# Edge buckets of 250 destinations instead of 417, and a new order at the seam of query stage, mask and first attention

## The chip, the cores and the metric

The kernel runs on one core of a Trainium2 chip. A core has four compute engines that run side by side and meet at semaphores: TensorE (PE, matmuls; PEld is its weight load), VectorE (DVE), ScalarE (ACT) and GpSimd (POOL). SyncE (SP) only issues DMAs here. The metric is the device time of one launch in microseconds (us). A median of several runs is given, beside one execution that was profiled.

## What is computed

One layer of a graph network over 1250 nodes of width 768 and 20000 edges, followed by a mixture of experts. Cut to what matters:

```python
xn = layernorm(x)
# 1. two graph attention layers over the edges, every node also has a self loop
def gat_conv(x, src, dst, W, a_src, a_dst, bias, H, C, n):
    h = (x @ W).reshape(n, H, C)
    e = leaky_relu((h * a_src).sum(-1)[src] + (h * a_dst).sum(-1)[dst], 0.2)
    ee = exp(e - segment_max(e, dst)[dst])
    alpha = ee / segment_sum(ee, dst)[dst]
    return segment_sum(alpha[:, :, None] * h[src], dst).reshape(n, H * C) + bias
gnn = concat([xn, gat_conv(gat_conv(layernorm(xn), 4 heads), 2 heads)]) @ Wu + bu
# 2. linear attention with q, k = elu(.) + 1, 12 heads
kv = einsum('bhsd,bhse->bhde', k, v); z = 1 / einsum('bhsd,bhd->bhs', q, k.sum(-2))
mix = (einsum('bhsd,bhde->bhse', q, kv) * z) @ w_proj + b_proj
x = x + gnn + mix
# 3. experts: 2 of 8 per node, and a shared one
x = x + ffn(layernorm(x))
```

## The kernel before

The nodes are laid out in NT = 10 tiles of T = 125. The program is written out by hand: each engine's code is a list in its own order, and semaphores (s_...) tie the lists. Nothing is scheduled by a planner, so the order of a line in the code is the order on its engine.

**Edges become a table of counts.** The graph attention here works on a dense matrix: counts[source, destination] holds how many edges join two nodes. To build it, the edges are sorted into buckets. A bucket is a tile of sources and a range of G destinations; with DG = 3 ranges G is 417, and NBK = NT * DG = 30 is the number of buckets. Sorting needs each edge's rank in its bucket. DVE writes one-hots of the bucket (onehot, line 1888), PE sums them, DVE forms bases (base0, base1, edge_bases), and edge_rank adds one-hots and bases with three or four bf16 matmuls for RC = 16 of 160 edge columns at a time; DVE multiplies and reduces the result (lines 1942, 1945). Then edge_slots makes slots, GpSimd scatters half of the edges to a table in memory (line 1260), and table_onehots with table_products do the other half on DVE and PE. Every bucket is filled up to whole chunks of 128 edges, which makes at most NCH = 186 chunks.

**The counting.** count_edges(n) stands in the code of PE and of DVE between other work. For each chunk PE multiplies a one-hot of sources (ohs) with one of destinations (ohd), 128 x G, into bank 6 or 7 (line 1393); DVE adds it to the bucket's place in counts (line 2055) and writes the one-hots of the chunk after the next (chunk_onehots, lines 2043 and 2045). s_cps, s_acc and s_ohb tie the two.

**Stages in order.** Keys and values (K/V, lines 1365 and 1375, with edge_work after each half group of twelve f32 passes; every f32 matmul appears as two passes), W1 times W2 (w12_product, 24 counts), the products of layer 1 (H1, line 1457, 80 counts), the query stage (line 1512, 30 blocks mb of six matmuls; for each row tile t attend, line 1475, DVE's normalise, and turn_mix, line 1501). At its end come the last two row tiles. Then the mask: ACT turns the counts of a source tile into floats (line 1787), PE transposes them (line 1564) and DVE writes MASKED where there is no edge (line 2178). Side units (line 1550) are 80 products with w_proj and Wu that fill PE's time in the mask and in the heads; DVE takes each result (take_sides, line 2171), SP brings its rows of x and sends the sums out. In the heads DVE takes maxima (largest, line 2194), ACT sends the destination rows to memory and back to all partitions (abbuf, send_rows), and per tile DVE and ACT form the weights (lines 1797, 2249, 1810, 2218) that PE multiplies (line 1589). AHEAD = 6 maxima of the next head are taken before the first tile; maxima(n, st) says how many after each tile.

## Time and profile before

| what | us |
|---|---|
| runs: median of 3 (lowest, highest) | 1655.09 (1655.03, 1657.01) |
| the profiled execution, its own time | 1648.37 |
| its span in the profile | 1646.6 |
| PE busy | 1540.9 (94%) |
| DVE busy | 818.1 (50%) |
| ACT busy | 322.0 (20%) |
| POOL busy | 252.6 (15%) |

The profiled execution is some 7 us shorter than the median of the runs, so a sum is made against 1648.37 and then carried over to 1655.09. Busy shares are averages over unlike stages: what a change in one stage is worth is read in that stage. The granted clock is full (1.00, the 2.4 GHz level) nearly everywhere.

### The profile page before, as it was taken

To read this page: it belongs to the slowest core of one execution; us is meant where nothing else is said; L and a number is where in the kernel's file an instruction comes from. 1 tells how busy PE (TensorE), PEld (TensorE's weight loads), DVE (VectorE), ACT (ScalarE), POOL (GpSimd) and SP (SyncE) were. 2 spreads that over 40 slices of the span, in tenths; PEclk is the share of its full clock that TensorE was granted. 3 is DMA by queue.
4 is the path that set the end of the run, shared out by engine and by line. 5 is a ranking of instruction groups with operands and counts; after the bars stand their busy time and mean duration, and the time that the engine had idled before them with its cause. 6 is when DMAs were issued, how large, how long until landed. Compare 5 with 4: busy or idle time off the path is not lost.

```text
span 1646.6 us, 21916 instructions
## 1 busy us (share of the span) xinstructions
PE 1540.9 (94%) x8496; PEld 1024.6 (62%) x8497; DVE 818.1 (50%) x1541; ACT 322.0 (20%) x481; POOL 252.6 (15%) x236
## 2 busy tenths in 40 slices
PE   3999999999898999999989999999999999999994
PEld 3566666557777899999877555444444444444441
DVE  7765347998875799994897433111111111111111
ACT  2111112001223145570273210100000100000000
POOL 1087820000000000000000027111111111111111
PEclk9999999999999999999999999999999999999997
DMA  8900020000003533323111317925628211614315
GB/s 224 380 2 2 2 61 1 1 1 2 1 1 102 148 101 132 88 55 69 46 46 58 144 36 172 336 69 188 221 62 306 95 49 48 215 42 160 98 30 187
DMA packets 84441, 163.79 MB, mean 99 GB/s; under 512 B 18746, under 2 KB 47152, under 8 KB 84105
## 3 DMA queue, kind: packets, MB, share of 16 engines
q1 hardware_dynamic: 65975, 119.07, 22.2%
q0 software_dynamic: 12128, 23.27, 6.1%
q10 hardware_dynamic: 6258, 20.40, 4.4%
q8 instruction: 48, 0.79, 0.2%
q14 instruction: 32, 0.26, 0.1%
HBM read 127.75 MB, written 37.56 MB: 100 GB/s over the span
## 4 chain that ended last, share of the span: by engine, by line
PE 70%; DVE 11%; DMA 8%; issue 4%; SPq 3%; POOL 1%; DVEq 1%; ACT 1%; ACTq 0%; POOLq 0%
PE bank L787 28%; PE bank L1589 5%; PE bank L1550 5%; PE bank L1365 5%; PE bank L1375 5%; PE bank L1457 5%; PE bank L1512 3%; PE bank L697 2%; SPq L368 2%; DVE arena L2249 2%; PE bank L1393 2%; DVE arena L2218 2%; DMA arena<-out_dram,arena 2%; PE bank L1637 1%; DMA arena<-in_x_dram 1%
## 5 line engine op out<-in xcount | busy, mean ns | idle before, releaser
L787 PE MATMUL bank<-arena 128*64 128x384 f32 x3312 | 539.4, 487 | 0.6 <-ACT arena L855 0.6
L787 PEld LDWEIGHTS bank<-arena 128*64 128x64 f32 x3312 | 237.1, 137 | 291.0 <-issue 290.1
L1130 DVE SCALAR_TENSOR_TENSOR arena<-bank,arena 64x384 f32<-64x384 f32 x92 | 52.6, 611 | 379.8 <-DMA arena<-out_dram,arena 232.9
L1589 PE MATMUL bank<-arena 125*125 125x198 f32 (+1 forms) x1200 | 188.8, 316 | 11.5 <-DVE arena L2218 11.4
L1589 PEld LDWEIGHTS bank<-arena 125*125 125x125 f32 x1200 | 181.8, 191 | 16.4 <-DVE arena L2218 16.2
L1550 PE MATMUL bank<-arena 128*125 128x192 f32 x960 | 163.0, 327 | 10.4 <-DVE arena L2171 8.7
L1550 PEld LDWEIGHTS bank<-arena 128*125 128x125 f32 x960 | 155.9, 188 | 12.4 <-DVE arena L2171 10.2
L1260 POOL DMA_INDIRECT slot_table<-arena x80 | 110.4, 1380 | 105.1 <-DMA expert_in<-arena 75.7
L2055 DVE TENSOR_TENSOR arena<-arena,bank 125x417 f32 x186 | 109.4, 588 | 27.5 <-PE bank L1393 19.0
L2249 DVE SCALAR_TENSOR_TENSOR arena<-arena 125x1250 f32<-125x1250 f32 x60 | 90.9, 1516 | 11.6 <-ACT arena L1797 11.6
L654 POOL MEMSET arena<- 1x2500 f32 x1 | 2.2, 2179 | 603.4 <-DVE arena L2201 603.4
L1457 PE MATMUL bank<-arena 128*125 128x396 f32 x240 | 92.9, 496 | 0.0
L1810 ACT ACTIVATE arena<-arena 125x1250 f32<-125x1250 f32 x60 | 74.7, 1245 | 85.5 <-DVE arena L2249 84.2
L1512 PE MATMUL bank<-arena 128*128 128x250 f32 x360 | 89.7, 374 | 1.7 <-DVE arena L2108 1.7
L684 POOL DMA_INDIRECT out_dram<-arena x46 | 42.1, 916 | 308.1 <-DVE arena L1130 308.1
L2194 DVE CUSTOM_DVE_ANT_0 arena<-arena 125x1250 bf16<-125x1250 bf16 x60 | 86.6, 1455 | 3.9 <-DMA arena<-score_rows 3.9
L864 ACT ACTIVATE arena<-bank 128x384 f32<-128x384 f32 x46 | 22.6, 492 | 333.6 <-PE bank L787 333.6
L2218 DVE SCALAR_TENSOR_TENSOR arena<-arena 125x1250 f32<-125x1250 f32 x60 | 87.2, 1454 | 0.9 <-PE bank L1589 0.9
L1797 ACT ACTIVATE arena<-arena 125x1250 f32<-125x1250 f32 x60 | 79.5, 1335 | 31.4 <-DMA arena<-score_rows 23.8
L1365 PE MATMUL bank<-arena 128*125 128x384 f32 x240 | 80.7, 488 | 0.0
L1375 PE MATMUL bank<-arena 128*125 128x384 f32 x240 | 80.4, 487 | 0.0
L1393 PE MATMUL bank<-arena 128*125 128x417 bf16 x186 | 64.7, 348 | 11.4 <-DVE arena L2045 11.2
(296 smaller groups left out, 1511.2 us busy)
## 6 DMA issues: line engine op xcount, KB each, us to landing
arena<-in_L_ffn_w_gate_dram SPq DMA_DIRECT2D x9, 2304.0 KB, 9.1
arena<-in_L_ffn_w_up_dram SPq DMA_DIRECT2D x9, 2304.0 KB, 10.5
arena<-in_L_ffn_w_down_dram SPq DMA_DIRECT2D x9, 2304.0 KB, 8.9
arena<-score_rows ACTq DMA_DIRECT2D x18, 585.9 KB
expert_in<-arena SPq DMA_DIRECT2D x23, 384.0 KB, 12.5
arena<-expert_in ACTq DMA_DIRECT2D x23, 384.0 KB, 3.3
arena<-in_L_mix_w_qkv_dram SPq DMA_DIRECT2D x3, 2304.0 KB, 24.1
xn_columns<-arena SPq DMA_DIRECT2D x1, 3750.0 KB, 14.1
```

Source lines behind the costliest of these rows:

```text
L787: ins = tp.matmul(ps[bank][HP * h:HP * h + HP, 0:384], frm[:, b, k, HP * h:HP * h + HP], ew[h][i][:, k, n * 384:(n + 1) * 384], start=(k = ...
L1260: pl.indirect_dma_start(table_dram[:, :], bass.IndirectOffsetOnAxis(ap=slot_i[0:T, c:c + 1], axis=0), vhw[0:T, NTB * TC + c:NTB * TC + c + ...
L1365: ins = tp.matmul(ps[hf][0:T, 0:384], xnT[:, k, t * T:(t + 1) * T], wkv[:, 0, k, hf * 384:(hf + 1) * 384], start=(k == 0), stop=(k == KD - 1))
L1375: ins = tp.matmul(ps[2 + hf][0:T, 0:384], xnT[:, k, t * T:(t + 1) * T], wkv[:, 1, k, hf * 384:(hf + 1) * 384], start=(k == 0), stop=(k == ...
L1393: tp.matmul(ps[6 + j % 2][0:T, 0:G], ohs[:, (j // OB) % 2, j % OB, :], ohd[:, j % 4, 0:G], start=True, stop=True).then_inc(s_cps, 1)
L1457: ins = tp.matmul(ps[q % 4][0:T, 0:2 * VW], xnT[:, k, t * T:(t + 1) * T], w12x[:, k, 2 * hf:2 * hf + 2, :], start=(k == 0), stop=(k == KD ...
L1512: ins = tp.matmul(ps[q % 2][:, 0:QN], wq[:, k, mb * P:(mb + 1) * P], xnT[:, k, g * QN:(g + 1) * QN], start=(k == 0), stop=(k == KD - 1))
L1550: ins = tp.matmul(ps[side_bank(u)][0:T, 0:FW], frm[:, k, t * T:(t + 1) * T], wchunk[:, c % 2, k, :], start=(k == 0), stop=(k == KD - 1))
L1589: ins = tp.matmul(ps[bank][0:T, c * width:(c + 1) * width], ptile[0:T, j % NPT, dt * T:(dt + 1) * T], values(n - first, st), start=(st == ...
L2055: dv.tensor_tensor(o, o, ps[6 + j % 2][0:T, 0:G], ALU.add).then_inc(s_acc, 1)
L2218: stt(out=ptile[0:T, j % NPT], in0=tbuf[0:T, j % NTB3], scalar=1.0, in1=counts[0:T, st, 0:N], op0=ALU.min, op1=ALU.mult).then_inc(s_pt, 1)
L2249: stt(out=tbuf[0:T, j % NTB3], in0=abbuf[0:T, n % 2, 1], scalar=ssrc[:, st:st + 1], in1=tbuf[0:T, j % NTB3], op0=ALU.add, op1=ALU.max).the ...
```

## The change

1. DG becomes 5, so a bucket has 250 destinations. There are 50 buckets and NCH = 206 chunks. edge_rank works on RC = 8 columns, 20 times. base0 moves to other memory. The bucket number is found by a multiplication and a shift.
2. In the K/V stage the ranks are placed in pairs, in the middle and at the end of the half groups from the third on. The clearing of the count table moves from DVE to ACT (t = 3), the W2 columns from g = 5, 6 to g = 30, 31, which are in t = 7. The W1 x W2 stage has three counts per product instead of two.
3. At the seam, attend of the last row tile uses banks 6 and 7 and no longer waits for normalise; both attends stand ahead of both turns; ACT converts the first tile of counts before the last copies of mixT and the second before the score rows' DMAs. Side units after the mask start in bank 7, and only the one in bank 5 waits for the whole mask.
4. In the heads DVE takes one more side unit ahead of the first tile, two at it, and fewer at the second; maxima moves one maximum from the first tile to a later one in heads 0 and 4.

```diff
-    DG = 3
+    DG = 5
...
-        rank_tmp = take(960).rearrange("p (i c b) -> p i c b", i=2, c=16)
-        RC = 16
+        RC = 8
         RJ = EC // RC
+        rank_tmp = take(2 * RC * NBK).rearrange("p (i c b) -> p i c b", i=2, c=RC)
...
-            return ((1, 1, 1, 1, 2, 1, 1, 2, 1, 1), (1, 1, 1, 1, 1, 0, 1, 0, 0, 0), (1, 2, 1, 1, 1, 0, 0, 0, 0, 0),
-                    (0,) * 10, (1, 1, 1, 1, 0, 0, 0, 0, 0, 0), (0,) * 10)[n][st]
+            return ((0, 1, 2, 1, 2, 1, 1, 2, 1, 1), (1, 1, 1, 1, 1, 0, 1, 0, 0, 0), (1, 2, 1, 1, 1, 0, 0, 0, 0, 0),
+                    (0,) * 10, (0, 1, 1, 1, 1, 0, 0, 0, 0, 0), (0,) * 10)[n][st]
...
+        def mix_bank(t):
+
+            return 6 if t == NT - 1 else 2
+
         def side_bank(u):
             n = sum(side_mask(st) for st in range(NT))
-            return 6 + u % 2 if u < n else 5 + (u - n) % 3
+            return 6 + u % 2 if u < n else 5 + (u - n + 2) % 3
...
+            def edge_ranks(i):
+
+                if 4 <= i < 4 + RJ // 2:
+                    edge_rank(2 * (i - 4))
+                    edge_rank(2 * (i - 4) + 1)
+
             def edge_work(g):
                 if g == 0:
                     edge_starts()
-                if 1 <= g < 5:
-                    for j in range(3 * (g - 1), min(3 * g, RJ)):
-                        edge_rank(j)
-                if g == 4:
+                edge_ranks(2 * g + 1)
+                if g == 6:
                     chunk_buckets()
...
+                        if k == KD // 2 - 1:
+                            edge_ranks(2 * (4 * t + hf))
...
                     w12_product(h, kp)
-                    count_edges(1)
+                    count_edges(2)
...
             def attend(t):
                 pe.wait_ge(s_qfeat, KD * (t // 2 + 1))
-                if t:
+                if t == NT - 1:
+                    pe.wait_ge(s_acc, NCH)
+                elif t:
                     pe.wait_ge(s_mixn, 2 * t)
...
             for t in range(NT - 2, NT):
                 attend(t)
+            for t in range(NT - 2, NT):
                 turn_mix(t)
...
+                    elif side_bank(u) == 5:
+                        pe.wait_ge(s_mask, 3 * NT)
...
-            pe.wait_ge(s_mask, 3 * NT)
...
+                if t == 3:
+                    act.wait_ge(s_rankfree, RJ)
+                    act.wait_ge(s_starts, 2)
+                    sc.activation(words(SMALL + COUNTS, CW16)[0:T], zeros[0:T, 0:1].to_broadcast([T, CW16]), ACT.Copy).then_inc(s_cz, 1)
...
+            act.wait_ge(s_acc, NCH)
+            act.wait_ge(s_diagc, NT)
+            act.wait_ge(s_qps, KD * NG)
+            count_floats(0)
             take_mixT(NT - 2)
             take_mixT(NT - 1)
-            act.wait_ge(s_qps, KD * NG)
+            count_floats(1)
             act.wait_ge(s_mixps, NT)
             act.wait_ge(s_spill, 16)
             score_row(0)
             score_row(1)
...
+            for st in range(2, NT):
+                count_floats(st)
...
-                if g in (5, 6):
-                    w2_columns(g - 5)
+                if g in (30, 31):
+                    w2_columns(g - 30)
...
                 for i in range(AHEAD):
                     largest_next(1)
-                    if i >= AHEAD - 4:
+                    if i:
                         take_sides(1)
...
                         if j == first * NT:
-                            take_sides(1)
+                            take_sides(2)
                         if j == first * NT + 1:
-                            take_sides(start_units[3] - 5)
+                            take_sides(start_units[3] - AHEAD - 1)
```

Three places show the new order. The first is PE's list in the K/V stage, from the V half groups on (before, 1308 to 1313 are a rank; 1375 is V):

```order
L1375 MATMUL bank<-arena 125x384 x6
L1308 MATMUL bank<-arena 125x480
L1309 MATMUL bank<-arena 125x480
L1313 MATMUL bank<-arena 125x480
L1308 MATMUL bank<-arena 125x480
L1309 MATMUL bank<-arena 125x480
L1313 MATMUL bank<-arena 125x480
L1308 MATMUL bank<-arena 125x480
L1309 MATMUL bank<-arena 125x480
L1313 MATMUL bank<-arena 125x480
L1375 MATMUL bank<-arena 125x384 x6
```

The same engine and place after (1314 to 1319 are a rank; 1387 is V):

```order
L1387 MATMUL bank<-arena 125x384 x3
L1314 MATMUL bank<-arena 125x400
L1315 MATMUL bank<-arena 125x400
L1319 MATMUL bank<-arena 125x400
L1314 MATMUL bank<-arena 125x400
L1315 MATMUL bank<-arena 125x400
L1319 MATMUL bank<-arena 125x400
L1387 MATMUL bank<-arena 125x384 x3
```

Three wide ranks after a half group have become two narrower ones after each half of it.

The second is PE's list at the seam, from the last but one attend to the first mask transpose, before:

```order
L1475 MATMUL bank<-arena 125x130 [waits mix_normalised,q_feature]
L1475 MATMUL bank<-arena 125x130 x5
L1501 MATMUL bank<-arena 128x125 [waits mixT_copied,mix_normalised]
L1501 MATMUL bank<-arena 128x125 x2
L1501 MATMUL bank<-arena 128x125 [waits mixT_copied]
L1501 MATMUL bank<-arena 128x125 x2
L1475 MATMUL bank<-arena 125x130 [waits mix_normalised,q_feature]
L1475 MATMUL bank<-arena 125x130 x5
L1501 MATMUL bank<-arena 128x125 [waits mixT_copied,mix_normalised]
L1501 MATMUL bank<-arena 128x125 x2
L1501 MATMUL bank<-arena 128x125 [waits mixT_copied]
L1501 MATMUL bank<-arena 128x125 x2
```

The same after (1491 is attend, 1517 the turn):

```order
L1491 MATMUL bank<-arena 125x130 [waits mix_normalised,q_feature]
L1491 MATMUL bank<-arena 125x130 x5
L1491 MATMUL bank<-arena 125x130 [waits chunk_counted,q_feature]
L1491 MATMUL bank<-arena 125x130 x5
L1517 MATMUL bank<-arena 128x125 [waits mixT_copied,mix_normalised]
L1517 MATMUL bank<-arena 128x125 x2
```

The second attend has moved ahead of the first turn, and its wait is on the counts and no longer on the normalisation.

The third is ACT's list at the same place, before (1727 copies mixT, 1746 are the score rows' DMAs, 1787 converts counts):

```order
L1727 ACTIVATE arena<-bank 128x3x125 [waits mixT_psum] x6
L1746 DMA arena<-score_rows 120x1250 [waits xnT_moved,rows_out,mix_psum,q_psum]
L1746 DMA arena<-score_rows 5x1250
L1746 DMA arena<-score_rows 120x1250 [waits rows_out]
L1746 DMA arena<-score_rows 5x1250
L1787 ACTIVATE arena<-arena 125x1250 [waits q_psum,self_loops,chunk_counted]
```

And after (1749, 1768, 1798):

```order
L1749 ACTIVATE arena<-bank 128x3x125 [waits mixT_psum] x2
L1798 ACTIVATE arena<-arena 125x1250 [waits q_psum,self_loops,chunk_counted]
L1749 ACTIVATE arena<-bank 128x3x125 [waits mixT_psum] x4
L1798 ACTIVATE arena<-arena 125x1250
L1768 DMA arena<-score_rows 120x1250 [waits rows_out,xnT_moved,mix_psum]
```

Two conversions have moved ahead of the four DMA issues, and the first of them ahead of the last four copies.

## Rows read from the trace of the kernel before

**Rows 1.** By stretch: length, busy PE, PEld, DVE, ACT, POOL; PEclk, DMA share, GB/s.

```profile
232.00:267.00 35.00, 29.57 (x173) 24.20 (x173) 29.89 (x70) 6.90 (x14) 0.00 (x0) 1.00 0.06 22
...
412.00:491.00 79.00, 71.14 (x387) 59.76 (x386) 62.74 (x155) 16.84 (x50) 0.00 (x0) 1.00 0.00 1
491.00:504.00 13.00, 6.17 (x47) 5.24 (x45) 3.25 (x9) 4.62 (x10) 0.00 (x0) 0.99 0.36 102
```

**Rows 2.** Timeline of the start: start us, us, engine, line, operation, [idle before].

```profile
8.95 1.15 DVE L1888 TENSOR_TENSOR arena<-arena 125x960 bf16<-125x960 f32 x1
...
24.83 1.94 DVE L1876 BATCH_NORM_STATS2 arena<-arena 125x6 f32<-125x384 f32 x4 [0.70 <-DMA arena<-in_x_dram]
```

**Rows 3.** Timeline of the ranking in the first K/V tiles.

```profile
39.27 5.14 DVE L1914 TENSOR_TENSOR arena<-arena 128x4800 bf16<-128x4800 bf16 x1
...
46.89 0.37 PE L1308 MATMUL bank<-arena 125*125 125x480 bf16 x1
...
54.05 0.37 PE L1308 MATMUL bank<-arena 125*125 125x480 bf16 x1
...
56.71 4.14 PE L1375 MATMUL bank<-arena 128*125 128x384 f32 x12
...
69.81 0.24 PE L1318 MATMUL bank<-arena 30*1 30x186 bf16 x1 [1.15 <-DVE arena L1942]
69.97 3.52 PEld L1365 LDWEIGHTS bank<-arena 128*125 128x125 f32 x12
```

**Rows 4.** Groups by line: busy us, mean ns of one, idle before.

```profile
L2055 DVE TENSOR_TENSOR arena<-arena,bank 125x417 f32 x186 | 109.4, 588 | 27.5 <-PE bank L1393 19.0 <-issue 5.3
...
L2045 DVE TENSOR_SCALAR arena<-arena 128x417 bf16<-128x417 f16 x186 | 60.8, 327 | 0.0
...
L1787 ACT ACTIVATE arena<-arena 125x1250 f32<-125x1250 uint16 x10 | 12.3, 1244 | 12.2 <-PE bank L1564 11.1 <-issue 1.2
...
L1942 DVE TENSOR_TENSOR arena<-bank,arena 125x480 f32<-125x480 f32 x10 | 6.5, 650 | 5.5 <-PE bank L1313 5.5
```

**Rows 5.** Timeline: last scatter on GpSimd, and DVE before the first W1 copy.

```profile
220.94 1.17 POOL L1260 DMA_INDIRECT slot_table<-arena  x1 [0.30 <-issue]
...
233.01 0.55 DVE L2068 COPY arena<-bank 96x384 f32<-96x384 f32 x1 [3.85 <-PE bank L1407]
```

**Rows 6.** Timeline of the H1 stage: a count between f32 passes.

```profile
340.78 0.34 PE L1393 MATMUL bank<-arena 128*125 128x417 bf16 x1
...
340.96 1.49 PE L1457 MATMUL bank<-arena 128*125 128x396 f32 x4
```

**Rows 7.** Timeline: twelve short f32 passes (one attend), and their weight loads by line.

```profile
473.15 1.49 PE L1475 MATMUL bank<-arena 128*125 128x130 f32 x12
...
L1475 PEld LDWEIGHTS bank<-arena 128*125 128x125 f32 x120 | 14.6, 187 | 1.4 <-DVE arena L2135 0.8
```

**Rows 8.** Groups by line: two widths of a PSUM operand on DVE.

```profile
L2171 DVE TENSOR_TENSOR arena<-arena,bank 125x192 f32<-125x192 f32 x80 | 27.5, 350 | 23.6 <-PE bank L1550 21.3 <-DMA arena<-in_x_dram 2.3
...
L2125 DVE TENSOR_TENSOR arena<-bank,arena 125x384 f32<-125x384 f32 x20 | 11.2, 558 | 0.7
```

**Rows 9.** Timeline of the query stage: two turns, three blocks apart.

```profile
443.74 0.81 PE L1501 MATMUL bank<-arena 125*128 125x125 f32 x6
...
456.17 0.80 PE L1501 MATMUL bank<-arena 125*128 125x125 f32 x6
```

**Rows 10.** Timeline of the seam, and of PE after the mask.

```profile
502.50 2.38 ACT L1787 ACTIVATE arena<-arena 125x1250 f32<-125x1250 uint16 x2 [1.16 <-issue]
...
503.88 4.00 PE L1564 MATMUL bank<-arena 125*125 125x125 f32 x20 [3.12 <-ACT arena L1787]
...
532.40 21.72 PE L1550 MATMUL bank<-arena 128*125 128x192 f32 x132 [1.68 <-DVE arena L2178]
```

**Rows 11.** Timeline: DVE in layer 1, PE in layer 2, at the first tiles.

```profile
568.98 0.35 DVE L2171 TENSOR_TENSOR arena<-arena,bank 125x192 f32<-125x192 f32 x1 [0.58 <-DMA arena<-in_x_dram]
...
812.76 2.21 PE L1550 MATMUL bank<-arena 128*125 128x192 f32 x12 [2.23 <-DVE arena L2171]
```

73 lines of the change are left out of this document (40 added, 33 removed).

## The prediction

> **What bounds the kernel now.** I first read the page's busy shares. TensorE (PE) is busy 94% of the span, so the question is where PE waits and what else it is given to do. Next come the busy times by stretch [rows 1]. The change touches what lies before about 880 us. The expert part from there on is left as it is, and I put it at nothing.
>
> Three things are to be seen. In 232 to 267 us (the products of W1 and W2, with 24 edge chunks counted between them) PE and VectorE (DVE) are both busy about 30 of 35 us: each waits for the other. In 412 to 491 us (query stage) PE is idle 7.9 of 79 us. In 491 to 504 us (the seam) PE works 6.2 of 13 us. From 74 to 232 us (slices 3 to 5 of the page) the page shows PE full, so what is added there is paid in full. So is the ranking at 47 to 70 us, where a rank takes PE 0.9 us.
>
> **Buckets of 250: what it adds.**
> - *Start.* Each of the five bucket one-hots grows from 960 to 1600 elements. 960 take 1.15 us [rows 2], so 640 more take 0.67 us at the 0.96 elements per ns that these figures give. DVE has a spare wait for x before four of the five pieces, 0.3, 0.9, 0.9 and the 0.70 us shown [rows 2]. They cover most of it: five one-hots and the short new arithmetic on indices come to 3.7 us, and by adding up the pieces against the landing of x, the last statistics start 0.5 us later.
> - *Bases.* base0 grows from 4800 to 8000 elements: 5.14 us becomes 8.6. base1, of 960 and then 1600, goes by the same rate from 1.0 to 1.7. The first rank can start some 4.1 us later. PE now wants it half a V group (1.9 us) later than before, so about 2.1 us of new waiting remain.
> - *Ranks.* There are 20 of 400 columns for 10 of 480. Three ranks in a row stand from 54.05 to 56.71 us [rows 3]: 0.89 us each, of which three matmuls of 480 columns are 0.60. With 400 columns the streaming is 0.50 and the 0.29 of gaps stay: 0.79. Twenty are 15.8 us. Four of them need a fourth matmul (0.7 in all), ten places instead of four pay the change of operand type (0.1 us each, 0.6 more), and the wait of 1.15 us before the chunk numbers [rows 3] stays. That is 18.2 us against 11.3 now, the stretch from 46.9 us (first rank) to 69.97 less three groups of 3.87: +6.9. If the gaps shrink too it is +5, if nothing shrinks +9.5. DVE needs 0.65+0.65 us per rank now [rows 4] and about 1.1 then, 2.2 per pair against 3.5 of PE, so it does not set the pace.
> - *Table.* 160 matmuls of 206 instead of 186 columns: 20 columns at 2.4 GHz are 8 ns, +1.3 us in a full stretch.
> Together +10.8 us up to the end of the K/V stage.
>
> **What lies beside other work.** The fill of the count table goes from DVE to ScalarE (ACT). 1250 elements take ACT 1.24 us [rows 4], so 6256 take about 5.7. PE first needs ACT again four half groups (15.5 us) later, so I cost it at nothing; a stall would start if it took over 12 us. The scatter of the table on GpSimd starts when the slots are known, about 6 us later; it ends at 222 us now, and DVE sits idle 3.85 us before the first W1 copy [rows 5]. PE arrives 10.8 us later, so this is covered with some 8 us to spare. The W2 columns move to t=7, where DVE is idle for 12 us at a time: nothing.
>
> **What it saves.** The counts go from 186 of 417 columns to 206 of 250.
> - *PE.* In the H1 stage a count takes 340.78 to 340.96 us, then the next f32 pass starts [rows 6]: 0.18 us, 417 columns at 2.4 GHz (granted clock 1.00 in rows 1). With 250 columns it is 0.104, but the load of f32 weights must fit beneath. Twelve passes of 130 columns take 1.49 us [rows 7]: a pass every 0.11 us, each with such a load. So a count costs 0.11, and 80 of them in the PE-bound H1 stage save 5.4 us.
> - *A rule against it.* The slot above follows the columns exactly [rows 6]. The Trainium skill (TensorE: Matmul & The Clock Gate, Back-to-back issue gap) says that in a stream with weight loads the spacing goes by both operations, 81 ns at 128 columns and 131 at 512. By that slope 167 columns fewer are worth 22 ns, and H1 would save 1.8 us. The row speaks for the columns.
> - *DVE.* An add is 0.588 us and a one-hot 0.327 for 417 elements [rows 4]. PSUM adds of 384 and 192 take 0.558 and 0.350 [rows 8]: 1.08 ns an element, so 250 take 0.41. The one-hot I put at 0.24. Adds and one-hots follow each other at 0.82 us a count now and at 0.57 then.
> - *W1 x W2 stage.* It gets 12 more counts. Per head DVE now has 6 x 0.82 and then 9 x 0.57, +0.2, and half a chunk one-hot (0.93) more: with the hand-overs +0.6 per head, +2.5 us. Bounds: -1, if only waits shrink, and +5.
> - *Query stage.* Three blocks of six query matmuls go with each attended row tile. They take 12.4 us, from the turn at 443.74 to that at 456.17 us [rows 9]. PE's own work in them is 36 f32 passes (7.5 us), 9 counts (1.57), one attend and one turn (1.97): 11.0. The rest is waiting for DVE's one-hots. Then PE's work is 10.5 and DVE's 3x(3x0.57+0.3+0.41)+1.5 = 8.8. DVE still lags in the block with the two normalisations (4.1 against 2.8 us), which I give 0.5 us per three blocks. The stage runs from 373.4 to 491.5 us, 118 in all. Then the six first blocks take 17.0 (72 passes and 18 counts) and eight trios 11.0 each, with all 90 counts in them: 105, so 13 us are saved. Bounds 10 and 17.
> Subtotal: 10.8 + 2.5 - 5.4 - 13 = -5.1.
>
> **The seam.** From the last query matmul (491.5 us) to the first mask transpose (503.88) are 12.4 us [rows 10]: attend 8, normalise, turn, attend 9, normalise, turn, copy, ACT's four DMA issues, and the conversion of the first counts (1.24). Attend 9 has banks of its own then and runs under normalise 8; the first conversion runs before the turns. Chain then: attend 8 at +1.35, attend 9 to +3.9, normalisations to +5.8, turn to +6.6, copy to +7.2. The transposes start at +7.3: 5.1 us saved. ACT's second conversion and the DMA issues end at +10, so the third tile starts at +11.4 where it starts at +16.5 now: the 5.1 survive. After the masks PE waits 1.68 us for bank 5 [rows 10]; the first side unit then goes to bank 7, 1.95 us long, and covers it. DVE's own chain to the first destination rows gains only part: -1.2.
>
> **First attention.** PE stands 2.2 us at 812.8 us before the ninth side unit [rows 11] and as much at 573.8, both times behind DVE's takes. With one more take ahead of the loop, two at the first tile and no maximum there, layer 2 gets 2 us earlier. In layer 1 DVE waits at 568.98 us for a row of x [rows 11] that stands in a queue behind the broadcast rows; an earlier take there only waits earlier, and holds the head's first steps. I take +0.2 there: together -1.8, between -6 and +2.
>
> **Sum.** -5.1 - 5.1 - 1.2 - 1.8 = -13.2 us. Against the profiled execution's own 1648.37 us (span 1646.6) that gives 1635.2. The runs shown have a median of 1655.09, 6.7 above it, so I predict 1641.9.
>
> **The rivals.**
> 1. *The count's slot stays 0.18 us*, set by the weight load of 187 ns [rows 7] and not by columns. Then H1 saves nothing, and in the query stage 90 counts keep 0.07 us each, so that it saves 7: 10.8 + 2.5 - 7 - 8.1 is -1.8, 1653.3. The pass every 0.11 us speaks against. Chance 0.08. By the Trainium skill's rule above a count would keep 0.048 us more than I take in H1 and the query stage, 170 x 0.048 = 8.2 us less gain, 1650.1; it shares this rival's chance, since the slot of 0.18 us at 417 columns is not what its slope gives.
> 2. *The early side units are eaten.* In layer 1 DVE stands at the first tile until the rows of x land behind the broadcasts, two takes in series, and PE's first attention matmul is not earlier than it is now: 6 us of the seam's gain are lost, 1647.9. For it: the wait for a DMA at 568.98 [rows 11]. Against it: the broadcasts start earlier as well. Chance 0.14.
> 3. *Slower: DVE's price of a count does not follow its width*, being hand-over, register load and semaphores. Then 20 more counts cost 16.4 us in the W1 x W2 and query stages, and nothing is saved there: 10.8 + 16.4 - 5.4 - 8.1 is +13.7, 1668.8. It decides where a count saves DVE under 0.11 us of the 0.25 that I take (16.4 - 126s = 2.7). The two widths in rows 8 speak clearly against. Chance 0.03.
> 4. *The change does not do what it says:* the maxima and waits of the mask tie the new order to the old moment, so that transposes start no earlier. The seam's 5.1 us are missing: -8.1, 1647.0. Chance 0.05.
> The forecast keeps 0.70.
>
> **How the numbers follow.** The terms' own bounds (ranks 4.5, W1 x W2 6, query 7, heads 8 us wide) put the forecast within about 8 us either side; rivals 2 and 4 lie inside, 1 and 3 outside. So 1633 to 1650. A measurement of this kernel tells 0.2%, 3.3 us, from no change. Faster by more: the forecast, rivals 2 and 4 and a little of rival 1, less an upper tail of 0.02, 0.88. Within: most of rival 1 and that tail, 0.09. Slower: rival 3, 0.03.
>
> **What would show it.** Right: ranks in pairs at about 0.8 us each and the K/V stage ending near 242 us; f32 passes 0.11 us behind a count; adds near 0.41 us; trios near 11 us; 7 us from the last query matmul to the first transpose; no wait of PE at the first side unit. Wrong: PE waiting for DVE in the ranks beyond 2 us, adds above 0.5, a stall of DVE on x at the first tile, or a lower granted clock at the seam.

## The result and the profile of the changed kernel

The changed kernel is slower. Five runs have a median of 1670.04 us (1665.38 to 1671.03); five runs of the kernel before beside them have 1656.55 us. The ratio is 1.0078, with a 95% interval from 1.0064 to 1.0091, so 11 to 15 us are lost where a gain of 13 was forecast. The profiled executions are 1671.03 us (span 1669.3) and 1648.37 us (span 1646.6), 22.7 us apart. That is more than the medians show, because the one of before is shorter than its timed runs and the one of after is the longest of its five. The table cuts the 22.7 us at the starts and ends of the stages' matmuls on TensorE. Its last row is code that did not change: 766.2 us there is the lowest of all 17 profiled executions, the others have 770 to 774.5, so most of those 6.5 us come from the one execution that before is read from.

| stage | before, us | after, us | difference | forecast |
|---|---|---|---|---|
| up to the end of K/V | 232.2 | 241.9 | +9.8 | +10.8 |
| W1 x W2, with 24 and 36 counts | 34.6 | 52.5 | +17.8 | +2.5 |
| bias products | 10.7 | 13.0 | +2.3 | 0 |
| H1, 80 counts | 95.9 | 90.4 | -5.5 | -5.4 |
| query stage | 118.4 | 111.3 | -7.1 | -13 |
| seam, last query matmul to first mask transpose | 12.1 | 7.9 | -4.2 | -5.1 |
| first mask transpose to first value product | 72.0 | 68.3 | -3.7 | -1.2 |
| heads, first to last value product | 304.5 | 311.3 | +6.8 | -1.8 |
| the rest (unchanged code) | 766.2 | 772.7 | +6.5 | 0 |

The largest loss is in the stage of W1 x W2, which moved seven times as much as forecast; the heads and the query stage miss the forecast by 9 and 6 us more. The windows of the changed kernel show it, one for the whole stage and one for its last 13 us (before: the first of [rows 1]); the second fence is what PE waits for longest there and, below it, the same in the kernel before (232.15 to 266.8 us), in us in total, times, longest:

```profile
core 0: us, PE busy (x) PEld busy (x) DVE busy (x) ACT busy (x) POOL busy (x), PEclk, DMA share, GB/s
241.95:294.40 52.45, 36.39 (x183) 29.34 (x181) 34.88 (x97) 6.90 (x14) 0.00 (x0) 0.85 0.00 1
...
281.50:294.40 12.90, 10.07 (x35) 8.60 (x35) 7.48 (x22) 0.50 (x1) 0.00 (x0) 0.52 0.00 0
```

```profile
PE bank L1407 <- DVE arena L2077: 14.9, 15, 1.7
...
PE bank L1393 <- DVE arena L2045: 2.6, 10, 0.4
```

Neither engine is full. PE works 36.4 of 52.5 us and DVE 34.9, and fifteen times PE waits for a one-hot (L2077) with a count (L1407), 12 us more in total than before. In the last 13 us the granted clock is 0.52, that is the level of 1.2 GHz. The page's groups that answer [rows 4], the add and the count:

```profile
L2087 DVE TENSOR_TENSOR arena<-arena,bank 125x250 f32 x206 | 85.1, 413 | 56.6 <-PE bank L1407 41.1
...
L1407 PE MATMUL bank<-arena 128*125 128x250 bf16 x206 | 58.2, 288 | 21.3 <-DVE arena L2077 21.1
```

An add takes 0.41 us, as forecast. DVE's timeline shows that it did not help. The rows are L2087 the add, L2077 the one-hot, L2100 the copy of the turned W1:

```profile
255.14 0.56 DVE L2100 COPY arena<-bank 96x384 f32<-96x384 f32 x1 [0.74 <-PE bank L1421]
255.96 0.41 DVE L2087 TENSOR_TENSOR arena<-arena,bank 125x250 f32 x1 [0.27 <-issue]
256.29 0.28 DVE L2077 TENSOR_SCALAR arena<-arena 128x250 bf16<-128x250 f16 x1
257.20 0.42 DVE L2087 TENSOR_TENSOR arena<-arena,bank 125x250 f32 x1 [0.63 <-PE bank L1407]
257.54 0.28 DVE L2077 TENSOR_SCALAR arena<-arena 128x250 bf16<-128x250 f16 x1
258.08 0.41 DVE L2087 TENSOR_TENSOR arena<-arena,bank 125x250 f32 x1 [0.26 <-issue]
```

From 257.20 to 258.08 are 0.88 us, of which add and one-hot fill 0.62. The other 0.26 is "issue", a gap without a semaphore. With 417 elements adds followed each other every 0.87 us too (first fence), but there the gap hid: the work alone needs 0.80 us, as a run without the range checks shows (e11 below, second fence).

```profile
255.41 0.59 DVE L2055 TENSOR_TENSOR arena<-arena,bank 125x417 f32 x1 [0.26 <-issue]
...
256.28 0.59 DVE L2055 TENSOR_TENSOR arena<-arena,bank 125x417 f32 x1
```

```profile
254.52 0.59 DVE L2068 TENSOR_TENSOR arena<-arena,bank 125x417 f32 x1
...
255.32 0.59 DVE L2068 TENSOR_TENSOR arena<-arena,bank 125x417 f32 x1
```

What fills the gap stands in the trace too, as instructions of DVE's queue (DVEq) that do not count as busy: the read of the bucket's offset into a register (TENSOR_LOAD), and two that check its range (FUSED_REGOPS, SEQ_ASSERT). Their times, lowest/median/highest in ns, are the same in both kernels (302, 190 and 23 ns), whatever the width:

```profile
L2082 DVEq TENSOR_LOAD <-arena x206: 296/302/551, 247.2 to 509.1; - x103
L2082 DVEq FUSED_REGOPS  x206: 190/190/206, 247.8 to 509.5; - x103
L2082 DVEq SEQ_ASSERT  x206: 23/23/35, 248.0 to 509.7; - x103
```

On PE the moment of DVE's timeline above reads (L1407 a count, L1421 the turn of W1, L1436 the product):

```profile
254.45 0.32 PE L1407 MATMUL bank<-arena 128*125 128x250 bf16 x1 [0.20 <-DVE arena L2077]
254.61 0.49 PE L1421 MATMUL bank<-arena 128*96 128x128 f32 x3
256.63 0.32 PE L1407 MATMUL bank<-arena 128*125 128x250 bf16 x1 [1.53 <-DVE arena L2077]
256.79 1.52 PE L1436 MATMUL bank<-arena 96*128 96x198 f32 x8
```

PE turns W1, then stands 1.53 us at the third count, and the next product stands behind that. In the same time DVE first waits for the turn (0.74 us), copies it, adds and writes the one-hot that the third count needs. The two engines take turns.

### The profile page after: what moved, and what is told of

The parts are those of the page before. It is cut to its first block, busy times and chain, and to the rows that moved or that the text cites. A ratio compares the mean times of both kernels' runs of the same rounds, so it can differ in the third digit from the quotient of the medians.

```text
span 1669.3 us, 22295 instructions
## 1 busy us (share of the span) xinstructions
PE 1561.1 (94%) x8588; PEld 1037.4 (62%) x8589; DVE 807.5 (48%) x1605; ACT 327.5 (20%) x482; POOL 253.0 (15%) x236
## 4 chain that ended last, share of the span: by engine, by line
PE 76%; DVE 11%; DMA 7%; issue 4%; ACT 1%; DVEq 1%; SPq 0%; ACTq 0%; POOL 0%; POOLq 0%
PE bank L792 29%; PE bank L1569 6%; PE bank L1607 5%; PE bank L1471 5%; PE bank L1387 5%; PE bank L1375 4%; PE bank L1528 4%; PE bank L702 2%; PE bank L712 2%; PE bank L730 2%; DMA out_dram<-arena 2%; DMA arena<-out_dram,arena 2%; DVE arena L2281 2%; PE bank L1655 1%; PE bank L1407 1%
## 5 line engine op out<-in xcount | busy, mean ns | idle before, releaser
L1607 PE MATMUL bank<-arena 125*125 125x198 f32 (+1 forms) x1200 | 194.0, 323 | 12.8 <-DVE arena L2250 12.5
L1607 PEld LDWEIGHTS bank<-arena 125*125 125x125 f32 x1200 | 187.6, 198 | 16.9 <-DVE arena L2250 16.8
L2087 DVE TENSOR_TENSOR arena<-arena,bank 125x250 f32 x206 | 85.1, 413 | 56.6 <-PE bank L1407 41.1
L2281 DVE SCALAR_TENSOR_TENSOR arena<-arena 125x1250 f32<-125x1250 f32 x60 | 90.8, 1514 | 9.1 <-ACT arena L1822 9.1
L1471 PE MATMUL bank<-arena 128*125 128x396 f32 x240 | 88.6, 497 | 0.0
L2250 DVE SCALAR_TENSOR_TENSOR arena<-arena 125x1250 f32<-125x1250 f32 x60 | 87.1, 1453 | 0.9 <-PE bank L1607 0.9
L1822 ACT ACTIVATE arena<-arena 125x1250 f32<-125x1250 f32 x60 | 79.6, 1335 | 30.9 <-DMA arena<-score_rows 23.5
L1407 PE MATMUL bank<-arena 128*125 128x250 bf16 x206 | 58.2, 288 | 21.3 <-DVE arena L2077 21.1
```

The lines of the kernel that those rows point to most:

```text
L1471: ins = tp.matmul(ps[q % 4][0:T, 0:2 * VW], xnT[:, k, t * T:(t + 1) * T], w12x[:, k, 2 * hf:2 * hf + 2, :], start=(k == 0), stop=(k == KD ...
L1607: ins = tp.matmul(ps[bank][0:T, c * width:(c + 1) * width], ptile[0:T, j % NPT, dt * T:(dt + 1) * T], values(n - first, st), start=(st == ...
L2087: dv.tensor_tensor(o, o, ps[6 + j % 2][0:T, 0:G], ALU.add).then_inc(s_acc, 1)
L2250: stt(out=ptile[0:T, j % NPT], in0=tbuf[0:T, j % NTB3], scalar=1.0, in1=counts[0:T, st, 0:N], op0=ALU.min, op1=ALU.mult).then_inc(s_pt, 1)
L2281: stt(out=tbuf[0:T, j % NTB3], in0=abbuf[0:T, n % 2, 1], scalar=ssrc[:, st:st + 1], in1=tbuf[0:T, j % NTB3], op0=ALU.add, op1=ALU.max).the ...
```

## The experiments

Each ratio is to runs of the kernel before on the same chip, with its 95% interval. The changed kernel itself has 1.0078.

**e1: the buckets alone**, with banks, waits, order, maxima and takes of the seam and the heads as before. Against the changed kernel, in part:

```diff
             for t in range(NT - 2, NT):
                 attend(t)
-            for t in range(NT - 2, NT):
                 turn_mix(t)
...
-                acc = ps[mix_bank(t) + b][0:T, 0:390].rearrange("p (k n) -> p k n", k=3)
+                acc = ps[2 + b][0:T, 0:390].rearrange("p (k n) -> p k n", k=3)
```

> The changed kernel with only the buckets of 250, their rank tables and the third count per product; the seam, the banks, the maxima and the early takes are those of the kernel before. The stages of the changed kernel's profiled execution differ from those of before by +9.8 us up to the end of K/V, +17.8 in the stage of W1 x W2, +2.3 in the bias products, -5.3 in H1 and -7.1 in the query stage: +17.5 together. Theory A (the loss is all in the buckets, the seam and heads part is a gain of 4 to 5 us): 17 us above before, about 1673. Theory B (half of the loss is in the reordered seam and heads): 8 to 10 us above before, about 1665.

Measured: 1672.15 us, ratio 1.0089 (1.0069 to 1.0110). It is 15 us above before, near the 17 of theory A: the loss is in the buckets.

**e2: the seam and heads alone**, with 186 chunks of 417. Against the changed kernel, in part:

```diff
-    DG = 5
+    DG = 3
...
-        RC = 8
+        RC = 16
```

> The kernel before (186 chunks, buckets of 417) with only the new order of query stage, mask and first attention. In the changed kernel the seam became 4.2 us shorter and the stretch from the first to the last value product 6.9 us longer, with a lower granted clock in it. Theory A (the longer heads are a chance of that execution's clock): 4 to 5 us faster than before, about 1652. Theory B (the new order of takes and maxima makes the heads longer): 2 to 3 us slower than before, about 1659.

Measured: 1653.36 us, ratio 0.9979 (0.9969 to 0.9990), 3.5 us faster than before and so near theory A. The seam is 7.4 us long and the first value product comes 8.9 us earlier, but the last layer takes 70.5 us from its first to its last value product where it takes 65.6 before and in e1. So this part of the longer heads is not a chance of the clock, and part of theory B holds.

**e3 and e4: four offsets read at once**, in the changed kernel and in the kernel before.

```diff
-                    off = dve.value_load(offs_i[0:1, j:j + 1], min_val=0, max_val=(NBK - 1) * G)
-                    o = counts_flat[0:T, bass.ds(off, G)]
+                    if j % 4 == 0:
+                        offs4[:] = nc.values_load_multi_w_load_instructions(
+                            offs_i[0:1, j:min(j + 4, NCH)], ...)[1]
+                    o = counts_flat[0:T, bass.ds(offs4[j % 4], G)]
```

> The changed kernel, with the bucket offset that VectorE reads into a register before each add read for four chunks at once, so 52 reads instead of 206. In the trace adds follow each other every 0.87 us in both kernels, although an add and a one-hot together fell from 0.87 to 0.61 us, and the gap of 0.26 us before the add shows no semaphore. Theory R (the read of the register sets the 0.87): three of four adds follow at 0.61 to 0.65 us, the W1 x W2 stage is 8 us shorter or more, and the granted clock does not fall in it; in all 12 to 18 us faster than the changed kernel, about 1654. Theory H (the hand-over between TensorE and VectorE sets it, two banks deep): cadence and time unchanged, about 1670.

> The kernel before with the same reading of four offsets at once (47 reads instead of 186). Here an add and a one-hot of 417 elements take 0.87 us by themselves, as long as the cadence. Theory R: the read is hidden under them, so next to nothing changes: 0 to 3 us faster, 1653 to 1656. If instead the read lay on top of the work in both kernels, it would gain as much as in the changed kernel, 10 us and more.

Measured: 1698.37 us, ratio 1.0262 (1.0243 to 1.0282), and 1689.20 us, ratio 1.0208 (1.0190 to 1.0226). Both are far slower, and my expectation was wrong. DVE's timeline of e3 says why (L2090 is the add here):

```profile
250.75 0.42 DVE L2090 TENSOR_TENSOR arena<-arena,bank 125x250 f32 x1 [1.98 <-issue]
251.08 0.28 DVE L2078 TENSOR_SCALAR arena<-arena 128x250 bf16<-128x250 f16 x1
251.38 0.42 DVE L2090 TENSOR_TENSOR arena<-arena,bank 125x250 f32 x1
...
252.01 0.42 DVE L2090 TENSOR_TENSOR arena<-arena,bank 125x250 f32 x1
```

Without a read and its checks between them adds are 0.63 us apart, so these do set the 0.87. But each of the four offsets keeps its own two checks, and the four reads come first, as one TENSOR_LOAD of 0.96 us (median of 52):

```profile
L2084 DVEq TENSOR_LOAD <-arena x52: 521/964/1218, 248.2 to 538.7; - x52
```

That is 0.24 us a value for 0.30, and from its end to the end of the last check are 1.11 us more (median), for 0.28 behind a single read. So the queue is hardly shorter in all, and it stands in one lump of 2.1 us, of which 1.98 are idle time here: one add and one-hot (0.62 us) cannot cover it, where single reads lie beneath an add each. The Trainium skill (DMA: Bandwidth & Descriptors, Latency and other measured facts) gives `tensor_load` a floor of about 600 ns and says that the compiler unrolls it four times to amortise it. By these rows a TENSOR_LOAD of one value is under that floor, and reading four at once saves a fifth of the reads' own time and loses the kernel 30 us.

**e5: two counts per product again.** The 12 counts go to H1.

```diff
                     w12_product(h, kp)
-                    count_edges(2)
+                    count_edges(1)
...
-                        if k not in (0, 3):
+                        if k not in (0, 3) or (k == 3 and q < 12):
```

DVE's lists change with it: two counts per product, five in each of the first 12 units of H1.

> The changed kernel with two counts per product in the W1 x W2 stage, as before, not three; the 12 counts taken out go to H1, a fifth one in each of its first 12 units. Theory D (VectorE sets the pace of the W1 x W2 stage at 0.87 us a count, and the clock falls because TensorE waits there): the stage takes 35 to 37 us again, not 52.5, the granted clock in it stays near 1.00, the bias products lose their 2.3 us, and H1 grows by 12 x 0.11 = 1.3 us as long as VectorE keeps up there: 17 to 18 us faster than the changed kernel, about 1653. Theory T (the stage is longer because narrower chunks or the table cost something of their own there): under half of it comes back, 1662 or more.

Measured: 1656.28 us, ratio 1.0002 (0.9992 to 1.0012). The stage takes 32.6 us at a clock of 1.00, less than before, and the bias products have no lower clock either. That is theory D for the stage; but H1 got 7 us longer and not 1.3. Five counts at 0.87 us, a result (L2140, 0.62 us) and the sources' one-hots take DVE about 5.3 us a unit, where PE needs 4.5 (90.4 us for 20 units in the changed kernel).

**e6: each product of W1 and W2 computed twice**, to keep PE busy.

```diff
-                for i in range(2):
+                for i in (0, 1, 0, 1):
```

> The changed kernel with each of the 12 products of W1 and W2 computed twice (eight matmuls more each, 1.36 us, 16 us of TensorE's work in all, no result changed), which lie in the 1.5 us that TensorE waits for VectorE in each group. Theory G (the granted clock fell to half after TensorE had waited for 40 us again and again): the clock stays near 1.00 through the stage and the bias products, and the kernel is 3 to 7 us faster though it does more. Theory N (the clock falls for another cause or costs nothing, since VectorE sets the pace): same time or up to 5 us slower, with the low clock at the same place.

Measured: 1676.18 us, ratio 1.0129 (1.0110 to 1.0148). The clock is 1.00 through the stage, but the stage takes 60.8 us. PE still waits 15.1 us for one-hots, as much as in the changed kernel (14.9). So the first half of theory G holds and the second doesn't: PE's added work lies in the chain with DVE and not in the waits, and what the clock costs can't be read from this run.

**e7: maxima of the last layer as before, in e2. e8: the seam alone, with all maxima and takes of the heads as before.**

```diff
-                    (0,) * 10, (0, 1, 1, 1, 1, 0, 0, 0, 0, 0), (0,) * 10)[n][st]
+                    (0,) * 10, (1, 1, 1, 1, 0, 0, 0, 0, 0, 0), (0,) * 10)[n][st]
```

> The kernel of e2 (before, with the new order of query stage, mask and first attention), but with the maxima of the last attention layer spread as before: one each at its first four tiles, not at the second to fifth. Its stretch from the first to the last value product of the last layer took 65.6 us in the kernel before and in e1, and 70.3 to 70.6 in the changed kernel, e2 and e3. Theory M (the last maximum of the second head comes one tile later, so its row returns 3 us too late for its first tile): 65.6 us again, in all 4 to 5 us faster than e2, about 1649. Theory S (the takes of side products moved ahead of the loop cause it): stays at 70, time as in e2, 1653.

> The kernel before with the new order at the seam alone (banks, waits, conversions, turns); maxima and takes of side products are those of before. Theory M or S: the last layer takes 65.6 us, and the seam's 4.9 us stay: 1651 to 1652 where e2 has 1653. If the takes ahead of the loop are worth the 3.8 us by which the stretch from the first mask transpose to the first value product is shorter in e2 and in the changed kernel, that stretch is 72 us here and not 68, and the kernel is no faster than e2; if they are worth nothing, 68 us stay.

Measured: 1648.68 us, ratio 0.9950 (0.9933 to 0.9967), and 1651.00 us, ratio 0.9967 (0.9952 to 0.9983). The last layer is back at 65.5 us in both. This is theory M, worth 4.7 us (e7 against e2). The changed kernel's DVE shows the mechanism (L2242 ends the destination row of the second head, L2250 weighs, L2281 begins a tile); below it is the only wait of DVE for ScalarE in that layer of the kernel before (L2249 begins a tile there):

```profile
841.97 0.17 DVE L2242 SCALAR_TENSOR_TENSOR arena<-arena 125x10 f32<-125x10 f32 x1
...
856.23 1.45 DVE L2250 SCALAR_TENSOR_TENSOR arena<-arena 125x1250 f32<-125x1250 f32 x1
860.97 1.52 DVE L2281 SCALAR_TENSOR_TENSOR arena<-arena 125x1250 f32<-125x1250 f32 x1 [3.28 <-ACT arena L1822]
```

```profile
844.72 1.52 DVE L2249 SCALAR_TENSOR_TENSOR arena<-arena 125x1250 f32<-125x1250 f32 x1 [1.17 <-ACT arena L1797]
```

and ACT's timeline the reason for its wait (L1758 takes the row, L1760 and L1778 are its DMAs, L1822 begins a tile):

```profile
849.98 0.27 ACT L1758 ACTIVATE arena<-bank 20x125 f32<-20x125 f32 x1 [2.06 <-PE bank L1506]
850.28 0.30 ACTq L1760 DMA_DIRECT2D score_rows<-arena  x1
...
851.96 1.05 ACTq L1778 DMA_DIRECT2D arena<-score_rows  x3
...
859.60 2.56 ACT L1822 ACTIVATE arena<-arena 125x1250 f32<-125x1250 f32 x2 [2.00 <-DMA arena<-score_rows]
```

The row goes out and comes back to all partitions only at 859.6 us. One tile fewer lies between the last maximum and the first tile of the second head. DVE waits for ScalarE twice in this layer, 1.2 and 3.3 us, where it waits once in the kernel before, 1.2 us.

**e9: the range checks left out. e10: and each offset read one add earlier.** The two instructions behind each read, FUSED_REGOPS and SEQ_ASSERT above, check its range. The value is clamped where it is computed, so they decide nothing. In e9 both are gone from the trace, and the read stays at 0.30 us.

```diff
-                    off = dve.value_load(offs_i[0:1, j:j + 1], min_val=0, max_val=(NBK - 1) * G)
+                    off = nc.values_load_multi_w_load_instructions(
+                        offs_i[0:1, j:j + 1], engines=[mybir.EngineType.DVE], min_val=0, max_val=(NBK - 1) * G,
+                        skip_runtime_bounds_check_because="offs_i was clamped to (NBK - 1) * G")[1][0]
```

> The changed kernel, with the two range checks left out that stand on VectorE's queue behind each read of an offset (the value is clamped when it is computed, so nothing else changes). e3 showed adds 0.63 us apart where no offset is read between them, and 2.26 us where four are read and checked, so one offset costs VectorE's queue some 0.5 us. Theory C (the checks are a large part of that): adds 0.75 us apart or less, the W1 x W2 stage under 48 us (52.5 with the checks), 8 to 15 us faster in all. Theory L (the read itself is the price): adds 0.80 to 0.87 us apart, 0 to 4 us faster.

> As e9, and each offset is read one add earlier than it is used, so that no instruction behind the read uses its value before the next add is through. Theory W (the queue stands still only where an instruction uses the value just read): adds 0.63 us apart, the W1 x W2 stage 43 us or less, and 10 us or more faster than e9. Theory Q (the queue stands in the read itself until it is answered): same cadence and time as e9, within 2 us.

e10 keeps a list and reads `offs[j + 1]` ahead of the add of chunk j:

```diff
+                    for m in range(len(offs), min(j + 2, NCH)):
+                        offs.append(...)
+                    off = offs[j]
```

Measured: 1662.09 us, ratio 1.0018 (0.9995 to 1.0041), and 1662.94 us, ratio 1.0018 (1.0000 to 1.0035). Theory C holds: 10 us by the ratios. Two adds of e9 in a row (L2089 here), then the window of the stage in e9 and in e10:

```profile
256.56 0.41 DVE L2089 TENSOR_TENSOR arena<-arena,bank 125x250 f32 x1
256.89 0.28 DVE L2077 TENSOR_SCALAR arena<-arena 128x250 bf16<-128x250 f16 x1
257.19 0.41 DVE L2089 TENSOR_TENSOR arena<-arena,bank 125x250 f32 x1
```

```profile
243.00:286.50 43.50, 29.85 (x182) 24.51 (x181) 35.09 (x97) 6.92 (x14) 0.00 (x0) 1.00 0.00 1
```

```profile
243.90:294.40 50.50, 37.10 (x182) 31.45 (x181) 35.01 (x97) 6.90 (x14) 0.00 (x0) 0.81 0.00 1
```

Adds are 0.63 us apart, as in e3 where no read lies between them, so the checks account for the 0.24 us and the read by itself is hidden. The query stage takes 106.2 us, against 111.3 in the changed kernel. Reading earlier brings nothing. That is the number of theory Q, but with the read hidden already e10 had nothing left to show: whether the queue stands still in the read or at its first use stays open. The two windows also price the clock, since the pace is the same in both. The 182 matmuls are the same; at 1.00 they are 29.9 us and at 0.81 they are 37.1, and the stage is 7 us longer. So e9's 43.5 us may not be set against the 52.5 of the changed kernel, whose clock was low: with the clock low in both (e10) the checks are worth 2.0 us in this stage.

**e11: e7 without the checks**, buckets of 417; the diff is that of e9.

> The kernel of e7 (buckets of 417, the new seam, maxima of the last layer as before), which took 1648.7 us, without the range checks. With 417 elements the cadence of 0.87 us is work (0.50 and 0.37), and the trace shows the read only as gaps of 0.26 us before the first add behind a copy. Under theory C these gaps close: 12 to 16 of them in the W1 x W2 stage and as many in the query stage, 0.1 to 0.26 us each, of which TensorE sees a part: 1 to 5 us faster, 1644 to 1648. Under theory L no change.

Measured: 1644.25 us, ratio 0.9919 (0.9905 to 0.9933), 13 us faster than the kernel before and 5 us faster than e7 by the ratios. So the checks cost the wide buckets something too: adds are 0.80 us apart without them, and the query stage takes 113.9 us for 118.4.

**e12: the changed kernel with the edits of e5, e7 and e9 together.**

> The changed kernel without the range checks (e9), with two counts per product and a fifth count in 12 units of H1 (e5), and with the maxima of the last layer as before (e7). From e5 (1656.3 us at that time's before of 1656.4): maxima 4.7 us, H1 7 us (VectorE no longer needs 0.87 us a count), query stage 5 us (e9 against the changed kernel): 1640, a ratio of about 0.990. If the forecast's gain of the narrow buckets is real once a count costs 0.63 us, this is 4 us faster than e11 (0.9919). If it is not, it is as e11 or slower, 0.992 to 0.995.

Measured: 1637.84 us, ratio 0.9885 (0.9868 to 0.9902). It beats both kernels, and e11 by 5 to 6 us in the ratios; the two profiled executions are only 2.4 us apart. The stage of W1 x W2 takes 29.5 us, H1 with 92 counts and the bias products 104.9 together, the query stage 106.2.

**e13: e9 with half of each product computed twice.**

```diff
-                for i in range(2):
+                for i in (0, 1, 1):
```

> The kernel of e9 with one half of each product of W1 and W2 computed twice (four matmuls more, 0.68 us, 8 us of TensorE's work in all, no result changed). Theory G (TensorE's waits in this stage bring the lower clock, and it costs 12 us): the slower group of times is gone or rare; times at 1650 to 1656 us in most executions, median 5 to 10 us below that of e9 (1662), granted clock 0.986 or more. Theory N (the clock falls by chance, whatever TensorE does there): two groups as in e9, each 0 to 4 us later, median 1662 to 1666.

Measured: 1663.37 us, ratio 1.0039 (1.0024 to 1.0054). That is not theory G's 1650 to 1656; the median is in the range of theory N, and against e9 the intervals overlap. In its profile the clock is 1.00 in the stage, which takes 50.0 us for e9's 43.5: PE waits 12.3 us for one-hots, as in e9 (12.5), and the 8 us more of PE's work go into the chain almost in full. The mean granted clock of its eleven executions is 0.983 to 0.989, in one group. In e9 seven of ten have 0.978 to 0.983 and take 1660 to 1665 us, and three have 0.988 or more and take 1648 to 1651. So a stage in which PE works more between the same waits keeps its clock, in e13 as in e6, and pays for it with the work. Why three executions of e9 kept the clock with the same program stays open; e10 (two of ten near 1654 us) and e1 (three of six at 0.983 or more) are split in the same way.

**e14: one call moved on DVE, in the changed kernel.** The first of the three adds stands ahead of the copies.

```diff
                     g = 3 * h + kp
+                    count_edges(1)
                     if g % 2 == 1:
...
-                    count_edges(3)
+                    count_edges(2)
```

> The changed kernel, range checks and three counts per product as they are, but in each group of the W1 x W2 stage VectorE makes the first of its three adds ahead of the copies of W1 x W2 and of the turned W1, not behind them. The one-hot of the third count is made behind that first add. Theory K (the third count closes a chain from the turns of W1 over their copy, the first add and the one-hot to the third count, and the next product stands behind it on TensorE: 1.2 to 1.7 us of waiting in 12 groups): the stage takes 36 to 44 us, not 52.5, the clock stays near 1.00, and the kernel is 9 to 17 us faster, 1653 to 1661. Theory P (it is the pace of VectorE alone, 9 counts of 0.87 us and the copies per head): 50 us or more, and at most 3 us faster.

Measured: 1657.18 us, ratio 1.0010 (0.9993 to 1.0027): 11 us faster than the changed kernel by the ratios. The stage takes 40.7 us at a clock of 1.00, with the checks in place and adds still 0.87 us apart, and no execution has a mean clock under 0.984 (the changed kernel: 0.977 to 0.982). PE's waits for one-hots in this stage, in e14 and in e9:

```profile
PE bank L1407 <- DVE arena L2077: 5.7, 16, 0.8
```

```profile
PE bank L1407 <- DVE arena L2077: 12.5, 16, 1.4
```

The waits go down with the order, and hardly with the pace (e9). Theory K holds.

**e15: e12 with the takes and the first layer's maxima as before.** In part:

```diff
-                    if i:
+                    if i >= AHEAD - 4:
                         take_sides(1)
```

> The kernel of e12 with the maxima of the first layer and the takes of side products ahead of and within the attention loops as in the kernel before (the last layer's maxima are so already). Theory X (these takes are worth the 1 to 4 us that the stretch from the first mask transpose to the first value product gained in e2): 1 to 4 us slower than e12, 1639 to 1642. Theory Y (what they gain there is given back in the first layer and between the layers, 1.5 and 1.8 us in e7 against e8): within 1.5 us of e12 or up to 3 us faster.

Measured: 1639.98 us, ratio 0.9909 (0.9887 to 0.9931). The intervals of e12 and e15 overlap, as those of e7 and e8 do. Both pairs lean to a gain of 2 to 4 us from the takes and the first layer's maxima, which change together in both; it is not settled.

## Why the prediction was wrong, point by point

- **Start, ranks, table: right.** First rank at 50.77 us, a wait of 1.59 us for 2.1, and a pair of ranks in 1.58 us, 0.79 each as forecast. The stretch grew by 9.8 us for 10.8. ACT's fill took 5.4 us and stopped nobody. Three figures of the working do not follow from what they name: 960 elements in 1.15 us are 0.83 per ns and not 0.96 (640 more did take 0.67 us), the stretch of ranks less three groups is 11.5 us and not 11.3, and 232.2 and 10.8 make 243 where the signs say 242.

```profile
50.77 0.38 PE L1314 MATMUL bank<-arena 125*125 125x400 bf16 x1 [1.59 <-DVE arena L1962]
...
52.35 2.20 PE L1387 MATMUL bank<-arena 128*125 128x384 f32 x6
```

- **The slot of a count on PE: right**, by the row and against the rule of the Trainium skill (TensorE: Matmul & The Clock Gate, Back-to-back issue gap) that stood beside it. From the count to the next f32 pass are 0.11 us (0.18 in [rows 6]), and H1 saved 5.5 us, not the 1.8 that the skill's slope gives. With it rival 1 is out:

```profile
342.08 0.27 PE L1407 MATMUL bank<-arena 128*125 128x250 bf16 x1
342.19 0.83 PE L1471 MATMUL bank<-arena 128*125 128x396 f32 x2
```

- **DVE's price of a count: wrong.** The step "Adds and one-hots follow each other at 0.82 us a count now and at 0.57 then" took the instructions' work for the pace and let it fall by 0.25 us. With the checks the pace was 0.87 us and stayed so, which the instructions on the queue set. Without them it is 0.80 for 417 elements (e11) and 0.63 for 250 (e9), a gain of 0.17: the add is 0.41 us as forecast, the one-hot 0.28 and not 0.24. That was the mechanism of rival 3, which I gave 0.03 because PSUM adds of two widths followed the width [rows 8]. Those adds read no register, so the rows did not bear on it. The sum of that rival, 1668.8, is near the result by luck. Its parts are not: the query stage did gain 7 us, and the W1 x W2 stage lost 18 with two more causes. In the query stage this term explains most of the miss. With 0.87 for 0.57 the prediction's own sum of DVE's work in a trio is 11.5 us and no longer under PE's 10.5, an estimate that gives 109 us for the stage. It took 111.3 us, and 106.2 without checks, where 105 were forecast. Even so the width alone was not worth 13: without checks the stage takes 113.9 us with 417 elements (e11), so 7.8 are the width's and the rest are the checks'. Three blocks from turn to turn took 12.6 and 11.4 us, forecast 11.0 (12.4 in [rows 9]):

```profile
449.65 0.81 PE L1517 MATMUL bank<-arena 125*128 125x125 f32 x6
...
462.27 0.81 PE L1517 MATMUL bank<-arena 125*128 125x125 f32 x6
...
473.62 0.81 PE L1517 MATMUL bank<-arena 125*128 125x125 f32 x6
```

- **The stage of W1 x W2: wrong by 15 us.** The step was "with the hand-overs +0.6 per head". It summed DVE's work and did not follow who stands behind whom. The third count waits for a one-hot behind an add behind the copy of a turn that PE makes just before. Moving one add (e14) took the stage from 52.5 to 40.7 us: PE's waits fell from 15.9 to 8.3 us, its busy time from 36.4 to 32.1. The longer busy time is the lower clock's: for the same matmuls at full clock it was 29.9 us in e9. The bias products, unchanged, took 2.3 us more behind it. In the profiled executions with fewer waits (e5, e12, e14) or with more work between them (e6, e13) the clock is 1.00 in the stage. That the waits bring the clock down is the likely reading and not a shown one, since three executions of e9 kept it. I had looked for a lower clock at the seam alone, where it stayed at 1.00.
- **The seam: right**, 4.2 of 5.1 us [rows 10], 4.7 in e2 and in e8. The transposes did start earlier, so rival 4 is out. The last query matmul ends at 509.06, the turns come at 513.93 and 515.32 and the transposes at 517.00:

```profile
510.76 2.93 PE L1491 MATMUL bank<-arena 128*125 128x130 f32 x24 [0.95 <-DVE arena L2167]
513.93 0.86 PE L1517 MATMUL bank<-arena 125*128 125x125 f32 x6 [0.24 <-DVE arena L2157]
515.32 0.86 PE L1517 MATMUL bank<-arena 125*128 125x125 f32 x6 [0.53 <-DVE arena L2157]
517.00 2.42 PE L1583 MATMUL bank<-arena 125*125 125x125 f32 x20 [0.83 <-ACT arena L1749]
```

- **The masks: a gain too small in the forecast**, 3.7 us for 1.2. Most of it comes with the seam alone (69.2 us in e8, 68.3 in the changed kernel). Rival 2's wait did come, which was one of the signs of being wrong: DVE stands 4.0 us at the first tile of layer 1 for a row of x, and 1.5 us at the next take. But its 6 us were not lost, since the first value product came 3.7 us earlier after the first transpose all the same:

```profile
578.57 0.35 DVE L2203 TENSOR_TENSOR arena<-arena,bank 125x192 f32<-125x192 f32 x1 [4.01 <-DMA arena<-in_x_dram]
```

- **The heads: wrong.** "no maximum there, layer 2 gets 2 us earlier" looked at the first tile and not at the last maximum, which moved one tile later and ends a row that has to travel to memory and back before the second head can start (e7, 4.7 us). The wait that I had seen at 812.76 us [rows 11] did go, and more than it came back at the second head. Of the 6.8 us, 4.7 are in the last layer, 1.6 in the first and 0.5 between them. Whether the 1.6 belong to the new takes is not shown: with them the first layer takes 180.7 to 183.5 us over the profiled executions, with the old ones 179.2 to 180.7.

## What to carry to other kernels

Take the pace of a repeated step from start to start and ask which queue sets it; a busy time says what a smaller tile saves only if the engine's queue has no register reads, checks or waits of the same length beside it. Before adding work to a stage in which two engines answer each other, write down for the new step what it stands behind on each queue, and put what the other engine waits for ahead of what waits for the other engine. A step that starts a round trip through memory is moved by the time to its last part, not its first.

## What the runs showed of the hardware

- Two range checks behind a register read keep VectorE's queue for 0.28 us (median of 206, from the end of the read to the end of the second check). From add to add they cost 0.07 us with 417 elements (0.87 against 0.80) and 0.24 with 250 (0.87 against 0.63). So they take away all that the narrower tile saves (0.17).
- The read itself, 0.30 us for one value, is hidden beneath an add and a one-hot (0.63 us from add to add with it in e9 and without it in e3). Reading four at once takes 0.96 us, and with their checks in one lump it left VectorE idle for 1.98 us and cost about 30 us in the whole kernel (ratios 1.0262 and 1.0078).
- TensorE at the 1.2 GHz level in a stage where it waits for another engine still costs: 7 us of 50 (e10 against e9), and 2.3 us more in the bias products behind it, where the lower clock held on (13.0 us for 10.7). One and the same program kept the full clock in three executions of ten and not in the other seven (e9, mean clock 0.988 or more against 0.978 to 0.983).
